# Attention and mixture of experts on one core: expert rows packed in blocks of 64

## The reference

```python
def ffn(x, gate_kernel, w0_kernel, w1_kernel, wo_kernel):   # x is the layer norm of the attention's sum
    gate_logits = jnp.einsum('bsd,de->bse', x, gate_kernel)
    top_k_weights, top_k_indices = jax.lax.top_k(gate_logits, 2)
    top_k_weights = jax.nn.softmax(top_k_weights, axis=-1)
    one_hot = jax.nn.one_hot(top_k_indices, 8)
    combine = jnp.einsum('bsk,bske->bse', top_k_weights, one_hot)
    h0 = jnp.einsum('bsd,edm->bsem', x, w0_kernel)          # 256 -> 512
    h1 = jnp.einsum('bsd,edm->bsem', x, w1_kernel)          # 256 -> 512
    inter = jax.nn.silu(h0) * h1
    return jnp.einsum('bse,bsem,emd->bsd', combine, inter, wo_kernel)   # 512 -> 256
x = x + xattn(layernorm(x), ctx, ctx)
x = x + ffn(layernorm(x), ...)
```

## Time and profile before

| what | value |
|---|---|
| median of 3 runs | 512.62 us (508.31 to 512.72) |
| profiled execution, its own time | 510.25 us |
| its span | 508.5 us |
| PE busy | 449.2 us, 88% of the span |
| DVE busy | 285.0 us, 56% |
| ACT busy | 239.4 us, 47% |
| POOL busy | 216.4 us, 43% |
| mean granted clock of PE | 0.925 of full |

### The profile page before, as it was taken

The page is one execution under the profiler, slowest core; times in us unless marked ns, Lnnn a source line. Parts: engine busy times, 40 slices in busy tenths (PEclk is TensorE's granted clock), DMA queues, the critical chain, the costliest instruction groups (busy, mean ns, idle before and its releaser), DMA issues.

```text
span 508.5 us, 10407 instructions
## 1 busy us (share of the span) xinstructions
PE 449.2 (88%) x3286; PEld 237.0 (47%) x3287; DVE 285.0 (56%) x603; ACT 239.4 (47%) x472; POOL 216.4 (43%) x235
## 2 busy tenths in 40 slices
PE   3938998988999989976589999999999999999991
PEld 3412343433443443332335665666666666656650
DVE  7898989888869889749884222222222222222220
ACT  2754987888768889744103222222222222222220
POOL 9574040536371513392331444444444444444422
PEclk9865999999979999967569999999999999999997
DMA  8776579688686725179920222322222322223321
GB/s 236 225 224 166 138 196 226 202 238 226 198 243 181 229 92 158 61 252 394 380 86 28 43 41 41 49 52 44 41 41 43 50 52 41 41 41 51 45 29 21
DMA packets 42331, 65.42 MB, mean 129 GB/s; under 512 B 6361, under 2 KB 32154, under 8 KB 42298
## 3 DMA queue, kind: packets, MB, share of 16 engines
q1 hardware_dynamic: 28570, 38.49, 27.0%
q0 software_dynamic: 11424, 24.39, 20.0%
q10 hardware_dynamic: 2304, 2.10, 1.3%
HBM read 40.18 MB, written 24.45 MB: 127 GB/s over the span
## 4 chain that ended last, share of the span: by engine, by line
PE 66%; DVE 14%; ACT 6%; DMA 4%; POOL 3%; issue 2%; ACTq 1%; POOLq 0%; SPq 0%; DVEq 0%
PE max_ps L1475 26%; PE pv_ps L1364 9%; DVE mx L916 7%; PE ring_ps L1487 6%; PE pv_ps L1487 6%; PE ring_ps L1347 5%; ACT pt L773 5%; PE max_ps L1223 3%; PE ring_ps L1447 3%; DMA Q<-mrow 2%; PE ring_ps L1244 2%; PE ring_ps L1437 2%; DVE K L1030 1%; POOL w_sb L596 1%; PE ring_ps L1330 1%
## 5 line engine op out<-in xcount | busy, mean ns | idle before, releaser
L916 DVE TENSOR_REDUCE mx<-max_ps 128x4 f32<-128x1024 f32 x128 | 150.1, 1215 | 19.1 <-PE max_ps L1223 19.1
L773 ACT ACTIVATE pt<-ring_ps 128x512 f32<-128x512 f32 x256 | 139.1, 598 | 31.7 <-PE ring_ps L1347 28.2
L1475 PE MATMUL max_ps<-w_sb,pt 128*128 x312 | 140.5, 593 | 0.9 <-ACT pt L837 0.9
L710 POOL DMA_INDIRECT out<-rb,sidx x39 | 62.0, 1591 | 119.9 <-DVE gidx L1161 58.5
L1186 DVE TENSOR_TENSOR pt<-pt,max_ps 128x512 f32<-128x512 f32 x39 | 26.8, 687 | 119.8 <-PE max_ps L1475 60.9
L1364 PE MATMUL pv_ps<-pt,w_sb 128*27 128x256 f32 (+2 forms) x1024 | 82.4, 407 | 0.7 <-ACT pvs L783 0.2
L1475 PEld LDWEIGHTS max_ps<-w_sb,pt 128*128 128x128 f32 x312 | 56.2, 190 | 57.1 <-issue 57.1
L1347 PE MATMUL ring_ps<-Q,K 50*128 50x256 f16 x512 | 53.1, 288 | 11.5 <-ACT pt L773 9.0
L1223 PE MATMUL max_ps<-K,Q 48*128 48x256 bf16 x512 | 53.5, 289 | 10.4 <-DVE mx L916 10.4
L844 ACT ACTIVATE pt<-ring_ps 128x512 f32<-128x512 f32 x39 | 23.3, 597 | 71.9 <-PE ring_ps L1447 71.9
L702 POOL DMA_INDIRECT pt<-xrow,gidx x39 | 38.7, 991 | 17.6 <-issue 11.8
(11 more groups left out here) (181 smaller groups left out, 444.4 us busy)
## 6 DMA issues: line engine op xcount, KB each, us to landing
w_sb<-in_L_ffn_w_kernel POOLq DMA_DIRECT2D x16, 512.0 KB, 8.1
K<-k_img SPq DMA_DIRECT2D x14, 448.0 KB, 6.3
Q<-q_img SPq DMA_DIRECT2D x14, 448.0 KB, 7.6
k_img<-kpart SPq DMA_DIRECT2D x28, 192.0 KB, 3.7
q_img<-qpart SPq DMA_DIRECT2D x28, 192.0 KB, 3.4
wo_sb<-in_L_ffn_wo_kernel POOLq DMA_DIRECT2D x8, 512.0 KB, 10.7
acc<-pvs SPq DMA_DIRECT2D x6, 512.0 KB, 3.0
q_sb<-in_x SPq DMA_DIRECT2D x16, 128.0 KB, 4.3
```

Source lines behind the costliest of these rows:

```text
L710: g.indirect_dma_start(xacc, bass.IndirectOffsetOnAxis(ap=sidx[sl.par][:, 0:1], axis=0), y_sb[sl.par], None, compute_op=ALU.add).then_inc( ...
L773: a.activation(pt[:, (2 * i + h) % PTN, :, :], bank(key)[:, :, :], ACT.Exp, scale=SCALE).then_inc(ring_read, 1)
L916: v.tensor_reduce(mx[:, t % 2, :, :, p].rearrange("q mt h -> q h mt"), max_ps[n % 2][:, :, :, :], axis=AX.X, op=ALU.max).then_inc(max_read, 1)
L1475: last = nc.tensor.matmul(flat(max_ps[sl.par][:, bank_of]), lhsT=xT[sl.par][:, k * P:(k + 1) * P], rhs=weight(w, e, KC, k), start=(k == 0) ...
```

## The change

The rows of an expert are rounded up to 64 and not to 128. Each expert then has a number of whole 128-row tiles and at most one leftover block of 64. Two leftover blocks of two experts share one tile (a mixed tile). At worst (4096 + 8 x 63)/64 = 71 blocks are needed, so NT is 36, of which NMIX = 4 are mixed: tiles 3, 7, 11 and 15. In a mixed tile rows 0 to 63 take the weights of one expert from SBUF as before. The weights of the other expert (512 KB each of w0, w1 and wo) are loaded again from memory into a staging buffer by SP, at an index read from `expert_of`; the first set behind `slots_done`, the others when the output of the mixed tile before is complete. A token whose two choices fall in the same mixed tile would be added twice by one scatter, so its second row is written out in a second scatter of that tile, `scatter_late`, with its own indices and weights.

In the routing, the part behind the ranks is done once for all 16 token tiles (`ranks` no longer ends with L1020 to L1025), the two early `onehots` calls are gone, all 32 one-hot matrices are written behind the last rank, PE's matmuls wait for each of them in turn, and the power on POOL becomes a reciprocal on DVE. The spare tokens are worked out by tile and not by expert.

```diff
-    NT = B * S * TOPK // P + E - 1
+    TAILS = (64,)
+    KINDS = len(TAILS) + 2
+    GRAIN = TAILS[-1]
+    PER = P // GRAIN
+    NT = ((B * S * TOPK + E * (GRAIN - 1)) // GRAIN + PER - 1) // PER
+    NMIX = (E * (PER - 1) + PER - 1) // PER
+    NTL = NT + NMIX
+    EVERY = 4
+    AFTER = EVERY * NMIX
+    STAGED = 3 * (PER - 1)
...
         def run_slots(engine, step):
-            for c in range(3):
+            for c in range(EVERY):
                 step(Slots(0, c))
-            with engine.Fori(0, (NT - 5) // 2) as i:
-                for c in (3, 4):
+            with engine.Fori(0, NMIX - 1) as i:
+                for c in range(EVERY, 2 * EVERY):
                     step(Slots(i, c))
+            for c in range(AFTER, AFTER + 2):
+                step(Slots(0, c))
+            with engine.Fori(0, (NT - 2 - AFTER - 2) // 2) as i:
+                for c in range(AFTER + 2, AFTER + 4):
+                    step(Slots(i, c, 2))
...
             sp.wait_ge(x2l_out, 48)
+            sp.wait_ge(rowl_out, 48)
+            sp.wait_ge(slots_done, 1)
+            sp.wait_ge(q_split, ST)
+            for j in range(NMIX):
+                if j > 0:
+                    sp.wait_ge(y_full, EVERY * j)
+                for c in range(1, PER):
+                    e = sp.value_load(expert_of[0:1, PER * j + c:PER * j + c + 1])
+                    for to, weights, n in ((w0_st, w0_view, KC), (w1_st, w1_view, KC), (wo_st, wo_view, FC)):
+                        sp.dma_start(to[c - 1], weights[:, bass.ds(e * n, n), :]).then_inc(staged, 16)
             sp.wait_ge(y_out, NT * 16)
+            sp.wait_ge(late_out, NMIX * 16)
...
-            g.wait_ge(norm_in, 1)
-            g.tensor_tensor(norm[:, :], norm[:, :], mone[:, :], ALU.pow).then_inc(norm_done, 1)
...
             def scatter(sl):
                 g.wait_ge(y_done, sl.t + 1)
+                if sl.step == EVERY and not sl.peeled and sl.c == EVERY + 1:
+                    g.wait_ge(late_out, (sl.i + 1) * 16)
+                elif sl.step == 2 and sl.c == AFTER + 1:
+                    g.wait_ge(late_out, NMIX * 16)
                 g.wait_ge(y_out, sl.t * 16)
...
+            def scatter_late(sl):
+                g.wait_ge(late_done, sl.j)
+                g.wait_ge(y_out, sl.t * 16)
+                g.sem_inc(pool_waited, 1)
+                g.indirect_dma_start(xacc, bass.IndirectOffsetOnAxis(ap=late_idx[:, 0:1], axis=0), late_sb,
+                                     None, compute_op=ALU.add).then_inc(late_out, 16)
...
                 if sl.has(-1):
                     scatter(sl.at(-1))
+                if sl.has(-2) and sl.at(-2).mixed:
+                    scatter_late(sl)
...
-                prod = num.rearrange("p u m -> p (u m)")[:, 0:TOPK * n * E].rearrange("p (k t e) -> p k t e", k=TOPK, e=E)
-                then(v.tensor_tensor(prod, A[:, :, to], before_t[:, None, to].broadcast_to([P, TOPK, n, E]), ALU.mult))
-                then(v.tensor_reduce(slot[:, :, to], prod, axis=AX.X, op=ALU.add))
...
-            onehots(0)
...
-            onehots(1)
...
+            then(v.tensor_tensor(len_i[:, :, :], total_i[:, None, :].broadcast_to([P, KINDS, E]), masks[:, :, :], ALU.bitwise_and))
+            then(v.tensor_copy(lens[:, :, :], len_i[:, :, :]))
+            v.tensor_tensor_scan(ends[:, 1:].rearrange(grains), lens[:, 1:].rearrange(grains), lens[:, 1:].rearrange(grains),
+                                 0.0, op0=ALU.add, op1=ALU.max).then_inc(chain, 1)
...
+            then(v.tensor_tensor(place, place, over[:, a], ALU.add))
+            then(v.tensor_tensor(picked, A[:, :, :, :], place[:, None].broadcast_to([P, TOPK, T, E]), ALU.mult))
+            then(v.tensor_reduce(slot[:, :, :], picked, axis=AX.X, op=ALU.add))
+            then(v.tensor_copy(slot_i[:, 0], slot[:, :, :]))
+            then(v.tensor_scalar(slot_i[:, 1], slot_i[:, 0], P - 1, None, ALU.bitwise_and))
+            then(v.tensor_copy(slot_f[:, 0], slot_i[:, 1]))
+            then(v.tensor_tensor(slot_f[:, 1], slot[:, :, :], slot_f[:, 0], ALU.subtract))
+            then(v.tensor_tensor(twice[:, :], slot_f[:, 1, 0], slot_f[:, 1, 1], ALU.is_equal))
+            then(v.scalar_tensor_tensor(slot_f[:, 1, 1], twice[:, :], float(NT * P), slot_f[:, 1, 1], op0=ALU.mult, op1=ALU.add))
...
-                v.tensor_tensor(onehot_t[:, k], slot_f[:, 1, k, :, None].broadcast_to([P, T, NT]),
-                                iota_t[:, None, :].broadcast_to([P, T, NT]), ALU.is_equal).then_inc(rows_picked, 1)
-                if k == 0:
-                    onehots(2)
+                v.tensor_tensor(onehot_t[:, k], slot_f[:, 1, k, :, None].broadcast_to([P, T, NTL]),
+                                iota_t[:, None, :].broadcast_to([P, T, NTL]), ALU.is_equal).then_inc(rows_picked, 1)
+                onehots(k, range(T))
...
+                    if done.mixed:
+                        v.tensor_copy(late_idx[:, :], row_of[:, bass.ds(NT + done.j, 1)])
+                        v.tensor_scalar(late_sb, y_ps[done.par][:, 0, :], wslot[:, bass.ds(NT + done.j, 1)], None,
+                                        ALU.mult).then_inc(late_done, 1)
...
-            keep_warm(3)
+            keep_warm(5)
...
+                    pe.wait_ge(told_done, n + 1)
...
-            keep_warm(1)
...
-            keep_warm(2)
+            keep_warm(3)
...
+                if sl.mixed:
+                    pe.wait_ge(staged, (sl.j + 1) * STAGED * 16)
+                for w, w_st, bank_of, full in ((w0_sb, w0_st, 0, h0_full), (w1_sb, w1_st, 1, h1_full)):
+                    if sl.mixed:
+                        for k in range(KC):
+                            for c in range(PER):
+                                rows = slice(GRAIN * c, GRAIN * c + GRAIN)
+                                last = nc.tensor.matmul(flat(max_ps[sl.par][rows, bank_of]),
+                                                        lhsT=xT[sl.par][:, k * P:k * P + P][:, rows],
+                                                        rhs=w_st[c - 1][:, k, :] if c else weight(w, e, KC, k),
+                                                        start=(k == 0), stop=(k == KC - 1))
...
+                if sl.mixed:
+                    for k in range(FC):
+                        for c in range(PER):
+                            rows = slice(GRAIN * c, GRAIN * c + GRAIN)
+                            last = nc.tensor.matmul(y_ps[sl.par][rows, 0, :], lhsT=interT[sl.par][:, k * P:k * P + P][:, rows],
+                                                    rhs=wo_st[c - 1][:, k, :] if c else weight(wo_sb, e, FC, k),
+                                                    start=(k == 0), stop=(k == FC - 1))
...
                 if sl.peeled and sl.t == 0:
+                    turn_spares()
+                if sl.peeled and sl.t == 1:
+                    spread_spares()
                     slot_weights()
```

More of the change, by code:

```diff
@@ L1067, in _ @@
             then(v.tensor_copy(token1f[:, :], token1[:, :]))
-            lead_e = E // 2
-            for i in range(2):
-                then(v.memset(ends[i][:, 0:lead_e], 0.0))
             residual_last(0)
@@ new lines, in _ @@
+            then(v.tensor_tensor(firsts[:, :, :], ends[:, 0:KINDS - 1], lens[:, 0:KINDS - 1], ALU.subtract))
+            v.tensor_tensor(place, before_t, firsts[:, 0, None, :].broadcast_to([P, T, E]), ALU.add).then_inc(chain, 1)
+            links[0] += 1
+            then(v.tensor_tensor(moves[:, :, :], firsts[:, 1:], ends[:, 0:KINDS - 2], ALU.subtract))
+            for a in range(len(TAILS)):
+                v.scalar_tensor_tensor(over[:, a], over[:, a], 0.0, moves[:, a, None, :].broadcast_to([P, T, E]),
+                                       op0=ALU.is_ge, op1=ALU.mult).then_inc(chain, 1)
+                links[0] += 1
```

262 lines of the change are left out of this document (151 added, 111 removed).

## The result

| | before | after |
|---|---|---|
| median of the runs, us | 512.6 (507.99 to 515.94, 20 runs) | 516.75 (510.73 to 522.58, 20 runs) |
| ratio to before | | 1.0074, 95% interval 1.0045 to 1.0104 |
| profiled execution: span, own time, us | 508.5, 510.25 | 514.5, 516.27 |
| expert tiles | 39 | 36 |
| first hidden matmul of the first and of the last tile, us | 268.15, 489.04 | 270.87, 495.31 |

A forecast was written before the change was run, and what follows sets the result against it. PE was taken to bound the expert tiles, and a chain of short DVE, PE and ACT steps the routing. 510.25 - 17.5 + 1.6 + 6.3 + 2.0 = 502.7 us; on the median 505.2 us, range 498 to 512.

The forecast's parts named there:

- part 4: Second scatter on POOL delays the next gather past its reserve of about 3 us; PE waits 1.4 us, four times.
- The prediction's last paragraph: Signs to check; prediction wrong if PE's sequencer, computing addresses for each half, falls behind or several gathers per mixed tile are late.
- the term of +6.3: Expert tiles: stalls behind the second scatter, four together 6.3 us, three of them 0.2 more for staged loads.
- the upper end of 2.4: Second scatter's stall if staged loads make the scatters come 1 us later: 2.4 us, three times.
- transfers collide: Rival: staged weights, scatters and gathers meet on the DMA engines; 3 to 5 us on top, 509 us; 20%.
- Fewer tiles: Expert tiles: 39 become 36 at 5.82 us each, 17.5 us less.
- The shape: Mixed tiles: halves run concurrently; changing in and out of column groups costs 0.1 us each, 1.6 us (0 to 4.8).
- Staged weights that PE waits for: Mixed tiles: SP's loads take about 7 us and are asked for earlier, so PE's wait costs nothing.
- The routing: Before the first tile: last logits 5.0 us sooner, but a longer chain and one-hots; first tile 2.0 us later.
- a whole tile's time of DVE: Spare and weight steps, moved behind the first tiles, have that much DVE time there; no cost in the sum.
- The attention: Before 221 us: touched only by five small POOL operations; costed at nothing, about 1 us if uncovered.
- a second scatter that is hidden: Rival: landing is quicker or the gather's reserve larger than read, so 6.3 us less, 499 us; 22%.

The follow-up runs named there:

- e8: Changed kernel with the late rows added to a separate buffer, so neither scatter waits for the other; 507.91 us, ratio 0.9841.
- e2: Changed kernel with staged weights loaded only once, so three mixed tiles reuse the first set; second scatter kept; 513.36 us, ratio 0.9991.
- e5: e3 with mixed tiles computed as plain ones, one expert's weights on all 128 columns; 497.68 us, ratio 0.9778.
- e3: Changed kernel without the second scatter and with staged weights loaded only once; 500.52 us, ratio 0.9751.
- e9: e6 with the slots' weights multiplied one step earlier, in the first tile's step, and without one wait; 501.95 us, ratio 0.9798.
- e1: Changed kernel without the second scatter of mixed tiles; staged loads kept; 503.56 us, ratio 0.9803.
- e10: Changed kernel with a plain tile's output matmuls reading weights at a fixed address; 514.97 us, ratio 1.007.
- e6: Changed kernel with each gather issued ahead of the scatters on POOL, plain scatter a step later, late scatter two; computes everything; 502.3 us, ratio 0.9856.
- e7: e6 with `keep_warm(1)` instead of `keep_warm(3)` ahead of the first tile; 502.68 us, ratio 0.9841.

## Why the prediction was wrong

**The step that failed** is in part 4: "PE wanted it at 7.78" and "about 3 us to spare". That point is where PE would turn the rows. The rows are wanted earlier, since PE's sequencer computes nothing further until they are there, and needs time for the output's addresses. In a plain tile the rows land 0.35 us after the hidden matmuls start. In the last stall of e8, which isn't at a mixed tile, they landed at 3.42 us and 1.71 were lost: they could have landed at about 1.7 us without loss. At its three others they landed at 3.2 to 3.4, and 1.0 to 1.5 us were lost beside the 0.2 of the shape, which gives 1.9 to 2.35. So the reserve was 1.4 to 2 us, where I read 3. The rest of part 4 held: late scatter 4.61 us behind the scatter (4.48 forecast), gather 1.87 behind that (1.87), rows turned 9.26 us behind the scatter (9.15). Without reloads the rows were 1.53, 1.47, 1.71 and 1.32 us late, for the forecast 1.4. Each stall was then 2.8 to 3.2, as lateness and 1.1 to 1.7 us for what stands behind it, the 0.2 of the shape with it. The prediction's last paragraph names the sequencer, but for the split matmuls of the mixed tile, where it did not fall behind; in part 4 it is missing.

**The second error, one of size,** is the staged loads in the same term. I took 0.2 us more for three of the four stalls, with 1 us as end. They moved the scatter of the first stall by 1.33 us (-3.08 us against -4.41 in e2), those of the next two by 1.3 and 0.9, and lateness with it: 2.75, 2.67 and 2.41 us. By the steps the loads are 4.5 us in all. So the term of +6.3 was 15.35 us: lateness 8.9 (2.75 + 2.67 + 2.41 + 1.05), and 6.5 of what follows it. All four stalls, 2.7 to 4.4 us, lie above the upper end of 2.4. The rival "transfers collide" had the place of this loss (3 to 5 us on top), and by itself would not have brought the time above that of before.

**The other terms, by the forecast's steps:**
- Fewer tiles, -17.5 us: held. In e5, with neither late scatter, reloads nor split, the first and the last tile's hidden matmuls start at 268.13 and 473.79 us, 15.2 us closer together than before, and 2.2 of the missing are the sum of its steps (1.96, -0.27 before). Its median of 497.68 us fits 512.62 - 17.5 + 2.0 = 497.1; its ratio, 0.9778, would make it 501.
- The shape, +1.6 (0 to 4.8): 2.34 us, or 0.15 a change for the 0.1 taken, as a mean over the 16. The halves run side by side, as the earlier trace rows had it. The Trainium skill, TensorEngine Tiling (Array Packing), section Key Properties, calls such a change a drain; at the pipeline's tail of 0.2 us it would be 3.2 us, and e3 and e5 lie halfway between.
- Staged weights that PE waits for, 0: held. The longest takes 7.3 us (the first `wo`), the median of the four is 6.1, and no PE instruction waits for them.
- The routing, +2.0: 1.5 from the first rank step to the first hidden matmul (41.55 us against 40.02). The chain before the first one-hot took 5.62 us for the forecast 5.7, the indices were there at 264.52 (264.1), the gather started at 265.67 (265.1), and PE turned the first rows at 269.57 behind `keep_warm`.
- Not in the sum: moving the weight steps behind the first tiles. I had given them "a whole tile's time of DVE", which they have; but PE waits for DVE's chain before the slot weights and comes to the output late. 1.8 us in the first two steps, which e9 takes back but for 0.1.
- The attention, 0: not shown otherwise. The 1.2 us there are less than its spread from run to run.

The sum with measured sizes: -17.5 + 2.3 + 15.35 + 1.5 + 1.8 = +3.5 us. In it 0.6 of the shape stands twice, since three stalls lie at mixed tiles. Missing are two short stalls. At 6-7 (0.78 us; 0.37 in e1, 0.09 in e3 without loads) it is the same failed step without any second scatter: the gather issued at 306.24, beside the loads, lands 5.1 us later, 3.00 us after the hidden matmuls start. PE turns its rows on time, and 0.7 us is lost beside the shape. In e8 the rows of that step landed at 3.80, and 1.58 were lost. At 16-17 (0.96 us) the clock is still at half for the first 1.4 us of hidden matmuls, and they take 0.66 us longer. With these it is +4.2 us, and the medians differ by 4.15. The 22% for a second scatter that is hidden rested on the same wrong reserve.

Why the clock falls in some stalls and not in others stays open: in the second stall it fell in e10 and stayed full in the changed kernel, after the same 2.44 us of idle time before L1529.

## What to carry to other kernels

Where an engine's sequencer stands still at a wait for data, as PE's does here, the data is due before the engine needs it: early enough for the address work that stands behind the wait. Read the reserve from the sequencer's records (here 1.4 to 2 of the apparent 3 us). Before a scatter that waits for another is put into a queue, look at what stands behind it: with the gathers issued first the same second scatter and loads cost 1.8 us (excess 6.07 against 4.30 with neither), and the kernel came out 7 to 10 us under the one before (e6, e9). And a loss can have two causes of equal length side by side; an experiment that removes one shows nothing until the other is gone too.

## What the runs showed of the hardware

- While PE's load waited for the gathered rows, PE's sequencer gave no record for 3.04 us (e8); computing one output matmul's address took 0.43 us, as long as one hidden matmul of 512 numbers.
- Eight 256-number output matmuls with fixed addresses took 1.89 us at full clock and 3.62 at half; with computed addresses, after a late wait, 2.07 at full and 3.26 at half clock, (the changed kernel), and 3.5 to the next hidden matmul either way.
- Two 64-column groups with weights and right-hand sides of their own, writing one bank, run side by side: 10 ns apart, 0.43 us a pair.
- Two scatters that depend on each other start 4.6 us apart; with 1.5 MB of loads beside them it was up to 7.5 (304.34 to 311.84 us). A gather landed 2.8 us after its issue, and 5.1 beside the loads.
- With one matmul of `keep_warm` ahead of the first tile and not three, the clock was at half until 277.4 us, and the first tile's hidden matmuls took 5.19 us instead of 3.69 (e7, e6).
